# Full attention of layer 2: how a block's negated row maxima reach the freed row of q

## The reference, cut to what matters

```
t = _to_tokens(x)                       # (2, 4096, 128)
t = t + _L2_attn_ref(_ln_t(t), ...)
    q, k, v = x @ w_query, x @ w_key, x @ w_value
    scale = einsum('bqd,bkd->bqk', q, k) / sqrt(128)
    probs = softmax(scale, axis=2)      # over 4096 keys, one head
    return einsum('bqk,bkd->bqd', probs, v)
```

## Time and profile before

| | us |
|---|---|
| median of 3 runs | 9185.72 |
| lowest and highest | 9179.64, 9197.97 |
| the profiled execution, its device time | 9173.38 |
| the profiled execution, its span | 9171.1 |

### The profile page before, as it was taken

How to read it: one execution, slowest core, us unless ns; L and a number is a source line. 1 busy time by engine, 2 the same in 40 slices (tenths; PEclk the granted TensorE clock), 3 DMA queues, 4 the chain that set the end, 5 groups by cost and what they waited for, 6 DMA issues and landing times. The chain is left out here.

```text
span 9171.1 us, 139845 instructions
## 1 busy us (share of the span) xinstructions
PE 8249.2 (90%) x42040; PEld 6698.1 (73%) x42040; DVE 7023.1 (77%) x7887; ACT 5757.1 (63%) x14820; POOL 6732.2 (73%) x3596
## 2 busy tenths in 40 slices
PE   6999999999999867899999999968999989888798
PEld 4766767677676633788888888855786868888775
DVE  6776767767677666899999999976777836999734
ACT  4877878778787734777777777731565623445304
POOL 3876868678696725899999999950686825999605
PEclk9999999999999977899999999988999989989898
DMA  2111111111111145544444444454000010000000
GB/s 93 28 40 30 41 40 30 41 28 44 26 42 33 56 170 202 149 104 108 107 105 110 104 107 108 106 184 151 29 23 18 23 53 19 1 1 1 20 8 19
DMA packets 480129, 596.14 MB, mean 65 GB/s; under 512 B 273736, under 2 KB 294480, under 8 KB 471568
## 3 DMA queue, kind: packets, MB, share of 16 engines
q1 hardware_dynamic: 479504, 588.17, 22.5%
HBM read 349.14 MB, written 157.03 MB: 55 GB/s over the span
## 5 line engine op out<-in xcount | busy, mean ns | idle before, releaser
L817 POOL TENSOR_TENSOR l_probs_low<-l_probs,l_probs_high 128x512 fp32r<-128x512 f32 x1792 | 2385.8, 1361 | 786.7 <-ACT l_probs_high L787 771.1
L1542 POOL TENSOR_TENSOR m_c_h<-m_h,m_c 128x2048 f32<-128x2048 f32 x520 | 2341.6, 4577 | 46.2 <-DVE m_h L1529 46.0
L1529 DVE TENSOR_TENSOR_SCAN m_h<-m_decay,m_ps_x 128x1024 f32<-128x1024 f32 x1040 | 2271.0, 2262 | 93.3 <-issue 69.3
L1442 PE MATMUL m_ps_y<-m_c_h,m_ident 128*128 128x256 f32 x8320 | 1977.9, 381 | 2.1 <-POOL m_c_h L1542 2.1
L873 DVE TENSOR_REDUCE l_max_by_row<-l_ps_all 128x8 f32<-128x512 f32 x2048 | 1357.9, 685 | 525.2 <-PE l_ps_all L636 446.3
L1442 PEld LDWEIGHTS m_ps_y<-m_c_h,m_ident 128*128 128x128 f32 x8320 | 1510.6, 190 | 173.1 <-POOL m_c_h L1542 3.7
L785 ACT ACTIVATE l_probs<-l_ps_all 128x512 f32<-128x512 f32 x2048 | 1240.5, 606 | 453.8 <-PE l_ps_all L677 310.1
L787 ACT ACTIVATE l_probs_high<-l_ps_all 128x512 fp32r<-128x512 f32 x2048 | 1233.0, 602 | 0.0
L2556 POOL TENSOR_TENSOR s_late<-s_late,s_products 128x1024 f32<-128x1024 f32 x352 | 858.3, 2481 | 314.6 <-ACT s_products L2538 314.5
L2096 POOL TENSOR_TENSOR l_probs_low<-l_probs,l_probs_high 128x512 fp32r<-128x512 f32 x512 | 664.8, 1305 | 566.0 <-ACT l_probs_high L2079 551.7
L1466 ACT ACTIVATE m_b_diagonals<-m_steps,m_b_rows 128x32 fp32r<-128x32 f32 x4160 | 966.8, 306 | 3.1 <-DMA m_b_rows<-b_t 3.1
(11 more groups left out here) (382 smaller groups left out, 13834.3 us busy)
## 6 DMA issues: line engine op xcount, KB each, us to landing
m_delta_u<-du_t SPq DMA_DIRECT2D x1040, 128.0 KB, 3.8
m_c<-c_windows SPq DMA_DIRECT2D x130, 512.0 KB, 4.3
l_q_and_row_bias<-l_q_parts SPq DMA_DIRECT2D x64, 512.0 KB, 5.1
du_t<-m_delta_u_high SPq DMA_DIRECT2D x128, 256.0 KB, 3.0
du_t<-m_delta_u_low SPq DMA_DIRECT2D x128, 256.0 KB, 2.9
ys<-m_y SPq DMA_DIRECT2D x256, 126.0 KB, 5.0
m_direction<-ys SPq DMA_DIRECT2D x12, 2048.0 KB, 14.4
l_xn<-xn SPq DMA_DIRECT2D x8, 2048.0 KB, 7.9
```

Source lines behind the costliest of these rows:

```text
L817: pool.tensor_tensor(pl[:, slot, :], pt[:, slot, :], f(ph[:, slot, :]), ALU.subtract).then_inc(low_pool, 1)
L1442: ins = pe.matmul(y_ps[:, group % 2, 0:DIRS * SPAN].rearrange("p (d t) -> p d t", d=DIRS), ident[:, :], ch[:, group % CH, :, n, :], start= ...
L1529: dve.tensor_tensor_scan(h[:, u % H, :], decay[:, pair % 2, ct, k % 2, :, :].rearrange("p n t -> p (n t)"), x_ps[:, u % X, :], 0.0, ALU.mu ...
L1542: pool.tensor_tensor(ch[:, group % CH, 2 * pair % DIRS:2 * pair % DIRS + 2, :, :].rearrange("p d n t -> p d (n t)"), h[:, 2 * pair % H:2 * ...
```

## The change

The four products, their wait and the copy from PSUM go. VectorE negates the 128 x 4 maxima into a new small tile `shift` right behind the reduction, at tile 25; SyncE writes it to a row of 512 floats in DRAM, waits for that to land, and loads the row into row 0 of q. TensorE's first score of a block waits for that load (`shift_in`). `fetch` moves from tile 29 to tile 25 on VectorE.

```diff
-    SUMS_AT, INVERSE_AT, FIRST, TURN_AT = 2, 4, 6, KT - 4
+    SUMS_AT, INVERSE_AT, FIRST = 2, 4, 6
...
+        shift = m.sb("shift", [P, QT], F32R)
...
-        turned, shifted = m.sem("turned"), m.sem("shifted")
+        joined, shift_out, shift_in = m.sem("joined"), m.sem("shift_out"), m.sem("shift_in")
...
+            def spread_shift(row):
+                cols = slice(row % NTB * TW, (row % NTB + 1) * TW)
+                sp.wait_ge(max_ok, row + 1)
+                if row:
+                    sp.wait_ge(shift_in, 16 * row)
+                sp.dma_start(shift_row.rearrange("a (k p) -> (a p) k", p=P), f(shift[:, :]), allow_slow_non_contiguous=True).then_inc(shift_out, 16)
+                sp.wait_ge(shift_out, 16 * row + 32)
+                sp.dma_start(f(qh[0:1, cols]), shift_row).then_inc(shift_in, 16)
+
+            sp.sem_inc(shift_out, 16)
...
                     sp.wait_ge(filled, (b + 1) * JOBS)
                     load(b + 1)
+                if j == 0:
+                    spread_shift(row)
                 tokens = slice(row * TW, (row + 1) * TW)
...
                 sp.dma_start(mraw[:, :, :, :], m_phi[row * P:(row + 1) * P, :]).then_inc(m_in, 16)
+                if j + 1 < NTB:
+                    spread_shift(row + 1)
                 if row >= 1:
                     before = slice((row - 1) * TW, row * TW)
                     sp.wait_ge(done, row)
...
-                def turn(row):
-
-                    pe.wait_ge(max_ok, row + 1)
-                    for k in range(QT):
-                        ins = pe.matmul(ps[:, MAX0, k * P:(k + 1) * P], mx[:, k:k + 1].to_broadcast((P, P)), ident[:, :], start=True, stop=True)
-                    ins.then_inc(turned, 1)
-
                 def score(row, queries, i, head=False):
                     if i == 0:
-                        pe.wait_ge(shifted, row + 1)
+                        pe.wait_ge(shift_in, row * 16 + 16)
...
-                            if i == TURN_AT:
-                                turn(row + 1)
...
-                turn(row0)
...
                     dve.wait_ge(max_taken, row * UNITS + UNITS)
-                    dve.tensor_reduce(mx[:, :], mx8[:, :, :], AX.X, ALU.max).then_inc(max_ok, 1)
-
-                def take_shift(row, j):
-
-                    dve.wait_ge(turned, row + 1)
-                    dve.tensor_scalar(qh[0:1, j * TW:(j + 1) * TW], ps[0:1, MAX0, :], -1.0, None, ALU.mult).then_inc(shifted, 1)
+                    dve.tensor_reduce(mx[:, :], mx8[:, :, :], AX.X, ALU.max).then_inc(joined, 1)
+                    dve.wait_ge(joined, row + 1)
+                    dve.wait_ge(shift_out, row * 16 + 16)
+                    dve.tensor_scalar(shift[:, :], mx[:, :], -1.0, None, ALU.mult).then_inc(max_ok, 1)
...
-                take_shift(it * NTB, 0)
                 fetch(TW)
...
                             if units_before(i) < UNITS <= units_before(i + 1):
                                 join_maxima(row + 1)
-                            if i == TURN_AT + 1:
-                                take_shift(row + 1, j + 1)
                                 if j + 2 < NTB:
                                     fetch((j + 2) * TW)
...
+    shift_row = dram("shift_row", 1, TW)
```

More of the change, by code:

```diff
@@ L1798, in _, with full_attention @@
                 finish(first + NTB - 1)
-def full_attention(nc, stage, xn, x, x_out, wq, wk, wv, ident_in, basis_in, matrices, m_phi, logits_in, gumbel_in, sigma_in, rank_in):
+def full_attention(nc, stage, xn, x, x_out, wq, wk, wv, ident_in, basis_in, matrices, m_phi, logits_in, gumbel_in, sigma_in, rank_in, shift_row):
     SCALE = float(P) ** -0.5
@@ L3087, in block_layers @@
     layer_norm(nc, "ln2", x2, xn2, a["channel_mean"], a["ident"], 1e-5)
+    shift_row = dram("shift_row", 1, TW)
     full_attention(nc, "l2", xn2, x2, x3, a["w_query_t"], a["w_key"], a["w_value"], a["ident"], a["basis"],
-                   matrices, a["m_phi"], a["log_weights"], a["gumbel"], a["sigma"], a["rank4"])
+                   matrices, a["m_phi"], a["log_weights"], a["gumbel"], a["sigma"], a["rank4"], shift_row)
     with Mem(nc, "stream") as stream:
```

## The result

| | before | changed |
|---|---|---|
| runs of the same session, median (lowest to highest) | 9182.68 us (9177.08 to 9197.97), 4 runs | 9331.02 us (9319.15 to 9341.07), 4 runs |
| ratio of the medians | | 1.0158, interval 1.0138 to 1.0179 |
| profiled execution, its span, its mean clock | 9173.38, 9171.1, 0.939 | 9341.07, 9339.5, 0.930 |
| the stage: issue of l_basis to issue of stream_x | 6406.92 to 7409.00: 1002.1 | 6424.28 to 7573.04: 1148.8 |

The change is slower by 148 us, 1.6%. The two profiled executions lie 168 us apart; 17.4 of that stand before the stage begins, where nothing was changed (runs of one kernel spread by some 20 us). The stage itself grew by 146.7 us, and that is the whole effect.

The account below looks back on a forecast made before the run. TensorE's own queue of products was taken to bound the loop; -12.6 (turn) + 1.4 (heads) + 1.4 (clock) = -9.8 us, so the profiled 9173.4 becomes 9163.6, or 9176 on the median; range 9165 to 9193.

Parts of the forecast that it names:

- the price of the write: Write of 512 floats to the DRAM row: 1.7 us, between 1.19 and 4.5, at 0.8 ns a piece.
- R: Time from the join's end to the first score that may start: 3.6 us, between 2.7 and 7.7.
- The load: Load of the row from DRAM into row 0 of q: 1.6 us, between 1.19 and 2.9.
- the clock after a stall in the loop: TensorE's granted clock after waits in the block loop: no term; a clock cost stood only at the two heads.
- The turn: TensorE's products that leave the loop: 0.90 us each, 14 in the loop, -12.6 us.
- the slack: In the loop, time from the join's end until the next block's first score needs the row: 5.6 us.
- the rule that turns R into time: In the loop each us of R beyond 5.6 costs 14; each of two heads costs R - 2.9.
- rival A: Slow write of 4-byte pieces, its wait replacing the turn: R 7.6, sum +26 us, 9212; chance 0.09.
- The negation and its wait: VectorE's negation of the 128 x 4 maxima after the join, with its wait: 0.23 us of R.
- its +1.4: Clock at the two heads, TensorE idle without the turn: +1.4 us for both, between 0 and 2.8.
- SyncE's and VectorE's work costs 0: Loop and heads: SyncE's delayed transfers and VectorE's negation and earlier fetch hold nothing up, cost 0.

## Why the prediction was wrong

It failed in the price of the write: the term stood at 1.7 us, at most 4.5, and the write took 8.4 to 10.6. By itself that step turns the sign: with 8.7 for the write and every other term as it was, R is 10.6 and the sum -12.6 + 14 x 5.0 + 2 x 7.7 + 1.4 = +74. The load was sized too low as well (about 2 us in each of 16 waits, +32), and the clock after a stall in the loop was a term at nothing. The turn, the slack and the rule that turns R into time held.

1. *The turn, 0.90 us a block.* Right: 53.42 against 53.43 forecast.
2. *The write, 1.7 us, at most 4.5.* Wrong, and the failed step: 8.7 (8.4 to 10.6). The price of a piece, 0.8 ns, was read off 64-byte pieces and carried to 4-byte ones, and the upper bound of 4.5 came from the same rows, so both ends of the range hung on one shape that doesn't have the effect. No row of before that the prediction read was a write in pieces so short and so close, and the bound should have said so by being open. The text did name, under rival A, that no row shows 4-byte pieces and that neighbouring partitions write to the same stretch; it was given 0.09.
3. *The load, 1.6 us.* Too low: 3.6 in the first head, 1.5 to 4.3 over all blocks. Alone it would be 1.3 to 1.4; up to 2.3 more come from reading freshly written short pieces, and 0.2 to 0.9 from the transfers behind it. The negation and its wait, 0.23 in the sum, were 0.33 in the heads and 0.67 in the block shown.
4. *R = 3.6, slack 5.6.* R was 12.8 to 13.6 in the loop, 12.4 and 12.5 in the heads. The slack was right: in the block shown TensorE's weight loads stand 7.73 us before the one at 6624.49, that is from 5.56 after the join's end. And the kernel whose R is 5.2 in the head doesn't wait in the loop, while the one with R at 6.2 to 6.5 waits 0.2 to 0.5.
5. *Beyond the slack each us costs 14, and in the heads 2.* Right, and incomplete. Between join and first score a block grew from 6.9 us to a mean of 13.3 over five blocks, +6.4, the 0.90 of the turn taken off already; the rule gives, with a mean R of 13.1 (the 0.19 of the join off), 13.1 - 5.6 - 0.9 = +6.6. From the first score to the next join it grew by another 2.3, which I had nowhere: 1.6 are the products at 1.2 GHz after each stall, 0.24 stand in every version with a transfer in place of the turn, 0.5 are open. The clock had been counted for the heads alone. There its +1.4 was of the right size: in the version with 16-byte pieces the stretches from an image's first join to its second grew by 2.8 and 2.7, of which R takes 2.3 and 1.6 and the slower pace 0.2 each, which leaves 1.1 for both.
6. *SyncE's and VectorE's work costs 0.* Right to 0.24 us a block, whose cause is open: 53.67 in the versions that keep all these moves and lose the slow write. But the DMA engines weren't free while the row travelled: the transfers that SyncE had held back go out right behind the load and make the DMA share 0.62 in the window from 6620.90, and they cost the load the 0.2 to 0.9 above.
7. *Rival A.* The kind and the sign were its own: the wait for the row takes the place of the turn, decided from R = 6.0. Its reason was wrong. It took the cost as one of pieces, four times that of 128; but 128 neighbouring pieces take 7.8 to 9.0 and 512 take 8.7 to 8.9, and 512 pieces 32 bytes apart take 1.9. With the measured R in its own formula, -12.6 + 14 x (13.1 - 5.6) + 2 x (12.4 - 2.9) + 1.4 = +113; the clock after 14 stalls (1.6 each), the 0.24 and the open 0.5 a block bring that to +146, of 146.7. That the sum closes so well proves little, since the 0.5 is itself what was left over in the loop.

The rule of the Trainium skill (DMA: Bandwidth & Descriptors, "Specifications") that the DMA engines do read-modify-write below 512 B warned in the right direction, but it doesn't tell the slow shape from the quick ones: 16-byte, 64-byte and 32-byte-spaced 4-byte pieces are under 512 B too and land in 1.4 to 2.0 us. The prediction wrote that by this rule rival A would be what happens, and that the trace agrees for 16 and 64 bytes; the rule has no price in it, and the rows show only that those two shapes are cheap, not how they are written. What the runs show is a cost of many short writes close together; that they are read-modify-writes queued at one place would fit, and no run shows it.

With the right price of the transfers the forecast's sum comes out: for 16-byte pieces R is 5.2 and 4.5 in the heads instead of 3.6, which costs 2.5, and 14 x 0.24 = 3.4 come on top, so -9.8 becomes -3.9; the stage of that kernel is 3.8 us shorter than before.

## What to carry to other kernels

A transfer's price goes by where its pieces land as much as by their number and size: write at least 16 bytes in one piece, or put the pieces 32 bytes apart, or stay in SBUF, before sending a column of words to a DRAM row. Where the nearest measured row has another shape of pieces, it bounds nothing from above, and the chance of the rival should say so. And a wait of 7 us in front of a busy TensorE costs more than its length, because the granted clock has to come back after each one (1.6 us here). Where what is written is read back at once, price the write and the read together.

## What the hardware showed that was not expected

- Neighbouring 4-byte writes to DRAM take 1.3 us for 16 words, 6.3 to 7.5 for 64 and 8.4 to 11.0 for 512. Into SBUF 128 of them take 1.9 to 2.0, and reading 512 of them from DRAM 2.1.
- In the changed kernel's trace the packets of the write are all done long before its landing is told. In a stretch of 9 us from 6611, its 528 packets lie in the slices at 6612.8 to 6613.3 (each digit 0.225 us), and the landing releases SyncE at 6620.9. (The 8 is one fetch of instructions.) Packet times alone would have put this transfer at 1.4 us.

```profile
DMA  0000000073000000000000008000000000000000
```

- A row written in 16-byte pieces is read back in 2.7 to 2.8 us right after its 1.4 us write, one written in 64-byte pieces or whole in 1.3 to 1.5. The waiting seems to move between write and read, with their sum near 4.0. The same holds for the 512 neighbouring words, with a sum of 12.0 in the free time and of 11.6 to 12.2 in the kernel when nothing follows the load; why the sum is the steady quantity no run shows.
- A stand of 7 us brings TensorE from granted clock 1.00 to 0.50, and the first eight products after it cost 1.6 us more.
